# Where six row-maximum passes and two final results stand in the head loop of a transformer block on one core

## The reference, cut to what matters

```
q, k, v = split(layernorm(x) @ w_attn + b_attn)     # 16 heads of 32; rotary factors by head on q and k
scores  = where(causal, q @ k.T, -inf)              # 512 x 512 per head
o       = softmax(scores) * E ** -0.5 @ v           # softmax needs each row's maximum
x1      = x + layernorm(o @ w_proj + b_proj)
h       = gelu(bitlinear(layernorm(x1), w_fc))      # 512 -> 2048, ternary weights
out     = x1 + layernorm(bitlinear(h, w_proj2))     # 2048 -> 512, ternary weights
```

## Time and profile before

| | |
|---|---|
| time, three runs | 1354.63, 1350.55, 1354.54 us; median 1354.54 |
| the profiled execution | 1356.18 us, of which the span is 1354.4 us |
| TensorE, matmul | 1202.9 us busy, 89% of the span |
| VectorE | 1015.4 us, 75% |
| ScalarE | 769.4 us, 57% |
| GpSimd | 595.7 us, 44% |
| mean granted TensorE clock | 0.948 |

### The profile page before, as it was taken

The page is one execution under the profiler, slowest core; times in us unless marked ns, Lnnn a source line. Parts: engine busy times, 40 slices in busy tenths (PEclk is TensorE's granted clock), DMA queues, the critical chain, the costliest instruction groups (busy, mean ns, idle before and its releaser), DMA issues.

```text
span 1354.4 us, 24946 instructions
## 1 busy us (share of the span) xinstructions
PE 1202.9 (89%) x9364; PEld 655.1 (48%) x9364; DVE 1015.4 (75%) x2931; ACT 769.4 (57%) x1414; POOL 595.7 (44%) x636
## 2 busy tenths in 40 slices
PE   4755879998999999998999999998999999988796
PEld 2322554455545554455545554554545554554352
DVE  7587797977787788967787777967787777777532
ACT  3334773665556664665566664665566655576470
POOL 6131342791149402881159312871159313971252
PEclk9865899999999999999999999999999999989798
DMA  5441121002310113002300212001300221001000
GB/s 202 129 152 64 27 76 56 1 4 54 101 33 2 42 46 102 1 18 58 105 12 2 56 50 83 1 24 50 111 7 3 56 59 44 2 1 55 9 1 32
DMA packets 49825, 65.37 MB, mean 48 GB/s; under 512 B 8581, under 2 KB 33189, under 8 KB 49192
## 3 DMA queue, kind: packets, MB, share of 16 engines
q1 hardware_dynamic: 49704, 63.77, 15.9%
HBM read 29.89 MB, written 8.39 MB: 28 GB/s over the span
## 4 chain that ended last, share of the span: by engine, by line
PE 50%; DVE 33%; ACT 5%; SPq 5%; issue 3%; DMA 2%; POOL 2%; POOLq 0%; DVEq 0%; ACTq 0%
PE gen L488 17%; PE down L531 15%; DVE score L1089 8%; PE score L557 4%; PE score L488 4%; DVE hT L950 4%; PE pv L585 3%; DVE gen L1089 3%; DVE probs L950 2%; SPq L397 2%; PE gen L548 2%; DVE mx L1089 2%; SPq L396 2%; PE score L563 2%; PE gen L483 1%
## 5 line engine op out<-in xcount | busy, mean ns | idle before, releaser
L809 ACT ACTIVATE probs<-score 128x512 f16<-128x512 f32 (+1 forms) x384 | 202.1, 526 | 133.4 <-PE score L557 133.4
L1423 POOL TENSOR_TENSOR rstd<-veps,mhalf 128x1 f32<-128x1 f32 (+1 forms) x104 | 67.4, 648 | 468.3 <-DVE veps L1166 349.9
L531 PE MATMUL down<-t2T,hT 128*128 128x512 f16 x1024 | 236.0, 384 | 13.7 <-DVE xn L1151 13.7
L950 DVE TENSOR_TENSOR probs<-score,probs 128x512 f16<-128x512 f32 (+1 forms) x384 | 213.6, 596 | 45.8 <-ACT score L811 45.1
L488 PE MATMUL gen<-x2T,t1T 128*128 128x512 f16 x1024 | 242.9, 383 | 4.0 <-ACT x2T L752 2.5
L811 ACT ACTIVATE score<-score 128x512 f32<-128x512 f32 (+1 forms) x384 | 205.0, 534 | 0.0
L488 PE MATMUL gen<-xT,wa 128*128 128x512 f16 x768 | 182.7, 390 | 20.9 <-DVE mx L1089 11.9
L1089 DVE CUSTOM_DVE_ANT_0 score<-score,mask_rows 128x512 f32<-128x512 f32 (+1 forms) x344 | 157.8, 521 | 0.0
L531 PEld LDWEIGHTS down<-t2T,hT 128*128 128x128 f16 x1024 | 97.0, 99 | 124.2 <-DVE xn L1151 16.3
L950 DVE TENSOR_TENSOR hT<-gen,hT 128x512 f16<-128x512 f32 x160 | 108.7, 685 | 53.4 <-ACT gen L772 27.5
L488 PEld LDWEIGHTS gen<-x2T,t1T 128*128 128x128 f16 x1024 | 95.4, 98 | 109.6 <-ACT x2T L752 5.2
(11 more groups left out here) (136 smaller groups left out, 1834.5 us busy)
## 6 DMA issues: line engine op xcount, KB each, us to landing
qk<-qkn SPq DMA_DIRECT2D x384, 64.0 KB, 2.0
xo<-x SPq DMA_DIRECT2D x8, 1024.0 KB, 5.3
hT<-x SPq DMA_DIRECT2D x8, 1024.0 KB, 6.5
out<-xn SPq DMA_DIRECT2D x32, 256.0 KB, 2.0
hT<-w_fc SPq DMA_DIRECT2D x4, 1024.0 KB, 6.7
hT<-w_down SPq DMA_DIRECT2D x4, 1024.0 KB, 5.4
hT<-w_attn SPq DMA_DIRECT2D x4, 512.0 KB, 10.2
hT<-w_attn SPq DMA_DIRECT2D x1, 1024.0 KB, 8.7
```

The lines of the kernel that those rows point to most:

```text
L531: mm = nc.tensor.matmul(down[:, :], hT[:, half, u, PARTS * tb:PARTS * (tb + 1)], t2T[:, u, :], start=(u == 0 and half == HI), stop=(u == F ...
L809: nc.scalar.activation(probs[:, h % 2, HI, 512 * i:512 * i + n], score[i][:, 0:n], ACT.Exp, scale=1.0 / S_UP)
L950: return V.tensor_tensor(out, whole, hi, ALU.subtract)
```

## The change

It alters two tables and the order of VectorE's work in a head. The six maxima move from heads 5, 6, 9, 10, 13, 14 to heads 8, 9, 11, 12, 13, 14 on TensorE and VectorE, and `general_plan` follows because it reads `STEP_MAX`. On VectorE the maxima keep their place before `probs_low` in heads 11 and 14 and stand behind `head_output` in heads 8, 9, 12 and 13. `final` of row blocks 1 and 2 moves from the start of heads 8 and 12 to the end of heads 6 and 10, with moments and terms right behind it. ScalarE's, GpSimd's and SyncE's lists are as before.

```diff
-FINAL_AT = {8: 1, 12: 2}
+FINAL_AT = {6: 1, 10: 2}
...
-STEP_MAX = {5: 0, 6: 1, 9: 2, 10: 3, 13: 4, 14: 5}
+STEP_MAX = {8: 0, 9: 1, 11: 2, 12: 3, 13: 4, 14: 5}
+MAX_FIRST = (11, 14)
...
-                    if prev and h in FINAL_AT:
-                        final(FINAL_AT[h])
                     if prev and here and h == SQUARES_AT:
                         hidden_variance()
                         final_terms(0)
                     if here:
-                        if nxt and h in STEP_MAX:
+                        if nxt and h in STEP_MAX and h in MAX_FIRST:
                             maxima(STEP_MAX[h], 1, in_general=True)
                         if h + 1 < HEADS:
                             probs_low(h + 1)
                         head_output(h)
                         if prev and h == HEADS - 2:
                             final(3)
+                        if nxt and h in STEP_MAX and h not in MAX_FIRST:
+                            maxima(STEP_MAX[h], 1, in_general=True)
                     if prev and h in FINAL_AT:
+                        final(FINAL_AT[h])
                         final_moments(FINAL_AT[h])
                         final_terms(FINAL_AT[h])
```

## The result

Over 20 runs each, the kernel after takes 1360.38 us (median; 1358.73 to 1361.93) and the kernel before 1354.64 us (1350.55 to 1361.18). The ratio is 1.0031, with a 95% interval of 1.0019 to 1.0043. The kernel after is slower: by 5.7 us between the medians, by 2.6 to 5.8 us going by the interval. I had forecast 6.1 us faster and a range that ended at 1355. Both the sign and the range were wrong.

The account below looks back on a forecast made before the run. TensorE was taken to be bound by waits in the head loop. Gains of 6.5 us (iterations 1 to 6) and 1.8 (iteration 0), less 2.2 (iteration 7), made 6.1 us: 1348.4 us against the median 1354.54, range 1341 to 1355.

Parts of the forecast that it names:

- What bounds the kernel: TensorE's waits in the head loop, at most about 4.6 us per iteration to win, ended mostly by VectorE's maxima and final results.
- Head 5 to head 7: Iteration 3: waits of 0.42 and 1.64 us go, a new 0.4 comes; TensorE is 3.71 us ahead at head 7.
- the replay: Iteration 3 worked out under the change from measured durations; gain 1.09 us per iteration, 6.5 over iterations 1 to 6.
- VectorE: ... head output 619.94: Head 6 of the usual iteration: after `probs_low(7)` at 619.14, the head output takes 0.80 us and ends at 619.94.
- The wait of 0.42 in head 5: TensorE's wait for the stacked queries and keys in head 5 goes, 0.42 us as in iteration 3.
- Third general bank: Maximum passes newly wait for `qk_low` to free their third bank: about 1, 2.0 and 0.5 us in heads 8, 11, 12.
- Iteration 7: No maxima there; `final` and moments delay scores(9) by 0.9 and down matmuls by 1.3: loss 2.2 us, bounds 0 and 3.
- Iteration 0: The 1.80 us wait for the pass that waits for DMA in head 5 goes: gain 1.8 us, bounds -1 and 4.
- The clock: The sum leaves the number of falls to 1.2 GHz at two: head 7's wait goes, waits in heads 11 and 12 come.
- The rival "slower": Waits of 2.0 and 0.47 us make the clock fall in head 12 every iteration: 1361.4 us, chance 0.10.

Follow-up runs that it names:

- e1: The kernel after with GpSimd's last addition narrowed to 8 of 512 columns in iterations 0 to 7; 1354.62 us, ratio to before 0.9988.
- e8: The kernel after with `final` and moments at their old places in iteration 7 only; 1355.67 us, ratio to before 0.9993.
- e10: As e1, with two GpSimd memsets of 352 columns each ahead of the narrowed addition; 1354.05 us in one run.
- e2: The kernel before with GpSimd's last addition narrowed to 8 of 512 columns in iterations 0 to 7; 1354.63 us, ratio to before 0.9997.
- e4: The kernel before with only the final results moved, the maxima left in their old heads; 1357.41 us, ratio to before 1.0015.
- e3: The kernel before with only the maxima moved, `final` and moments left at their old places; 1336.60 us, ratio to before 0.9857.
- e5: The kernel after with moments and terms back at the end of heads 8 and 12; 1339.85 us, ratio to before 0.9896.
- e6: e3 with ScalarE's part of the final results, and so GpSimd's addition, in heads 7, 10, 14 instead of 6, 9, 13; 1338.65 us, ratio to before 0.9885.
- e7: e3 with all six maxima in front of `probs_low`; 1333.40 us, ratio to before 0.9847.
- e9: e7, but in iteration 0 alone maxima 0, 1, 3 and 4 stand behind the head output; 1331.40 us, ratio to before 0.9827.
- e11: e7 with GpSimd's last addition narrowed to 8 of 512 columns; 1332.85 us, ratio to before 0.9834.

## Why the prediction was wrong

- **What bounds the kernel: right.** TensorE bound by waits in the head loop, with the waits at the places named.
- **Head 5 to head 7: right.** Head 7 began at 616.81; the replay had 616.69 + 0.12.
- **"VectorE: ... head output 619.94": the step that failed.** I took 0.80 us for a head output whatever GpSimd does. In head 6 of iteration 3 it took 1.58, as the product met the addition; in heads 9 and 13 about 1.74. This cost 0.90 us in head 8 and 0.88 at heads 14 and 15 (e1 against after). Without it the period is 148.71 us; my replay gave 149.58 - 1.09 = 148.49. So the hand-worked lists were right within 0.2 us, and the collision of product and addition was 1.8 of the 2.0 us per iteration by which I was off, 10.7 us over six. Rows that should have warned me were in the trace of before: the product of head 6 in iteration 7 took 1.20 us there, beside an addition. I put the wait of TensorE behind it down to VectorE's order alone.
- **The wait of 0.42 in head 5: wrong by iteration.** I took iteration 3 for all. In iterations 1, 5 and 6 the wait that went was 1.52, 1.01 and 1.07 us, which is 2.4 us of gain that my sum did not have.
- **Third general bank: right in kind and size.** 0.74, 1.89 and 0.36 us in heads 8, 11 and 12, where I had about 1, 2.0 and 0.5.
- **Iteration 7: right sign, too small.** I had 2.2 us, e8 shows 4.7. Scores(9) waited 1.9 us longer (2.48 for 0.56), which is the 1.91 us of `final` and moments in full. I had 0.9, which is what a head output of 0.80 in head 6 gives; it takes 0.9 more in both kernels (the same error). The down matmuls of head 9 ran longer at 1.2 GHz: 4.96 us, for 4.24 in the kernel before and 3.45 at 2.4 GHz.
- **Iteration 0: wrong.** I expected 1.8 us; its period is 151.95 us for 151.90. Heads 0 to 4 are 0.4 shorter and the head loop 0.8, and that is lost again behind scores(15): `values(0)` starts 4.60 us after it instead of 2.67, behind the pass of head 14, which waits 0.42 and 0.16 us for the maxima, and matmuls at 1.2 GHz (granted clock 0.71 for 0.82 before, over the 9.5 us from scores(15) on). I tested no change of it.
- **The clock: the falls moved, as the sum had it.** In the head loop two in the profile of before, in head 7, and two in that of after, in head 12 (1.7 us each, not 1.3); the wait before the fall of iteration 5 was 1.81 us, not 1.64; the profile of before has one more behind head 15. But e1 and e10 have four in head 12. The rival "slower" had its sign right and its mechanism only in part: the falls in head 12 come, but in 11 of 24 iterations, and are not what turned the sum.

In spans, after against before: iterations 0 to 6 and what precedes them 1.6 us longer, iteration 7 and the end 3.9 us longer, together 5.5. For iterations 1 to 6 alone I had 6.5 us of gain, and they lost 2.2. The difference of 8.7 is 10.7 for the collision and 1.3 for the replay, less 2.4 for the waits of head 5 and 0.9 for the clock, whose falls cost the profile of before 4.3 us there and that of after 3.4. That these two kept the loss small was luck, not forecast.

## What to carry to other kernels

Before moving work on VectorE, list for each of its instructions with two SBUF inputs what GpSimd reads at that moment, because a 0.29 us product can cost 1.2 us there, and two short chains that hang on the same event can meet in every iteration. Look through the whole trace for such an instruction that is at times longer than usual, and read a wait in every iteration before taking one for all. Put work of VectorE into heads where TensorE has long work of its own to cover it, and not in front of light ones. Try the halves of a change alone: here one half was worth 18 us by itself, and with the other added it was gone.

## What the runs showed of the hardware

- A VectorE product of 128x128 with both inputs in SBUF took 1.07 to 1.24 us instead of 0.29 when it began 0.2 to 0.35 us into a GpSimd addition of 1.26 us, and ended 0.15 us behind it. Beside a memset on GpSimd it took 0.29 (e10). VectorE's subtractions with one input in PSUM (128x512) kept their times beside the addition: 0.68 us there and 0.69 elsewhere, in the kernel before.
- Waits of 1.6 to 1.9 us cost TensorE its clock in some iterations and not in others, and no run shows what decides it. After head 7's wait of 1.64 us (1.81 in iteration 5) in before, e2 and e4, the following stretch ran partly at 1.2 GHz in 7 of 18 iterations. After head 11's wait of 1.89 us and the next of up to 0.31 (after, e1, e8, e10) it did in 11 of 24; e1 and e10, whose head loops are alike, had it in the same four iterations. In the six kernels whose waits in heads 5 to 14 are at most 1.03 us (e3, e5, e6, e7, e9, e11) it did in none of 36. Behind head 15 TensorE waits for VectorE's `xo`, in iteration 4 for 1.34 us and else for 0.99: there the clock fell in 5 of 13 profiles in iteration 4 (before, e1, e3, e9, e10) and never in the other 65 iterations.
- These falls show in the spread of the times. Of the 29 runs of before beside e1 to e4, the 7 with a mean granted clock of 0.948 or less took 1358.6 to 1362.2 us, all others 1357.6 or less. The 6 runs of e3 lie within 2.8 us.
